# Gelu from PSUM, clip within the fp16 split, maxima by scans: the feed-forward of a conv/attention hybrid on one core

## The reference

```python
def _quantize_activations_groupwise(x):          # NUM_GROUPS = 5, EPS = 1e-5, QB = 128
    n = x.shape[0]
    gs = n // NUM_GROUPS
    xq = jnp.zeros_like(x)
    for g in range(NUM_GROUPS):
        ag = x[g * gs:(g + 1) * gs]
        gamma = jnp.max(jnp.abs(ag))
        xq = xq.at[g * gs:(g + 1) * gs].set(jnp.clip(ag * QB / (gamma + EPS), -QB + EPS, QB - EPS))
    return xq

def _bitlinear(x, W, b):
    Wb = _binarize_weights_groupwise(W)
    y = jnp.einsum('btc,oc->bto', x, Wb) + b
    return _quantize_activations_groupwise(y)

h = _bitlinear(x, W1, b1)                        # 192 -> 768
h = jax.nn.gelu(h, approximate=False)
out = _bitlinear(h, W2, b2)                      # 768 -> 192
...
t = t + _L1_ffn_ref(_ln_t(t), ...)
```

## Time and profile before

| | |
|---|---|
| median of 3 runs | 5051.42 us (5050.09 to 5053.39) |
| span of the profiled execution, first to last instruction | 5053.9 us |
| busy, TensorE / VectorE / ScalarE / GpSimd | 4182.5 / 3623.6 / 2966.6 / 773.5 us |
| mean granted clock of TensorE | 0.940 |
| all DMA queues | 161.72 MB, about 14% of 16 engines' span |

### The profile page before, as it was taken

The page is one execution under the profiler, slowest core; times in us unless marked ns, Lnnn a source line. Parts: engine busy times, 40 slices in busy tenths (PEclk is TensorE's granted clock), DMA queues, the critical chain, the costliest instruction groups (busy, mean ns, idle before and its releaser), DMA issues.

```text
span 5053.9 us, 119820 instructions
## 1 busy us (share of the span) xinstructions
PE 4182.5 (83%) x38848; PEld 3015.4 (60%) x38848; DVE 3623.6 (72%) x8151; ACT 2966.6 (59%) x6655; POOL 773.5 (15%) x671
## 2 busy tenths in 40 slices
PE   4989887879889876989897779889876988897777
PEld 2666664556666545666664556666545666664555
DVE  3767678767777786777778667677775777678666
ACT  1555556846555575555566746555575555566745
POOL 0000002600000143000002600000153000002600
PEclk8999998989999998999998989999998999998989
DMA  2111111011121101111111011211101111111011
GB/s 64 33 33 33 34 38 26 0 45 33 38 53 33 33 0 38 33 33 39 33 33 26 0 45 38 46 40 33 33 0 38 33 33 39 33 33 26 0 38 39
DMA packets 46393, 161.72 MB, mean 32 GB/s; under 512 B 10098, under 2 KB 10612, under 8 KB 45684
## 3 DMA queue, kind: packets, MB, share of 16 engines
q1 hardware_dynamic: 45812, 154.38, 13.0%
HBM read 28.52 MB, written 25.17 MB: 11 GB/s over the span
## 4 chain that ended last, share of the span: by engine, by line
issue 78%; POOL 13%; PE 5%; DVE 2%; POOLq 1%; ACT 0%; DMA 0%; SPq 0%; DVEq 0%; ACTq 0%
POOL work L483 7%; POOL hi_z L453 1%; POOL hi_z L472 1%; POOL rstd L448 1%; POOL rstd L468 1%; PE S L662 1%; POOL NK L443 1%; PE OUT L649 1%; PE PT L734 1%; PE PT L630 1%; DVE nmax L1082 0%; PE S L670 0%; DVE work L339 0%; DMA B<-in_b 0%; PE S L616 0%
## 5 line engine op out<-in xcount | busy, mean ns | idle before, releaser
L841 ACT ACTIVATE work<-S,nmax 128x128 f32<-128x128 f32 (+7 forms) x1536 | 1138.8, 742 | 1119.0 <-DVE nmax L1082 1112.1
L1082 DVE TENSOR_REDUCE nmax<-S 128x1 f32<-128x128 f32 (+7 forms) x1536 | 1155.4, 753 | 620.3 <-PE S L618 574.5
L630 PE MATMUL PT<-ident,work 128*128 128x128 f32 x6912 | 1089.2, 282 | 270.5 <-DVE work L339 246.9
L630 PEld LDWEIGHTS PT<-ident,work 128*128 128x128 f32 x6912 | 752.4, 142 | 493.6 <-DVE work L339 291.5
L339 DVE COPY work<-PT 128x512 f32<-128x512 f32 (+3 forms) x1536 | 893.1, 581 | 25.1 <-PE PT L630 19.4
L662 PE MATMUL S<-odd,W1b 128*128 (+1 forms) x2160 | 526.9, 400 | 71.4 <-DVE work L1155 64.1
L483 POOL TENSOR_TENSOR work<-work 128x512 f16<-128x512 f32 x360 | 414.0, 1158 | 148.4 <-ACT work L887 120.1
L662 PEld LDWEIGHTS S<-odd,W1b 128*128 128x128 f16 x2160 | 214.1, 102 | 354.4 <-DVE work L1155 94.8
L616 PE MATMUL S<-KS,QS 128*128 128x512 f16 (+3 forms) x1152 | 335.9, 347 | 103.5 <-issue 60.9
L443 POOL TENSOR_TENSOR NK<-NK,halfneg 96x4 f32<-96x4 f32 x32 | 32.5, 1016 | 2200.7 <-DVE NK L1007 2200.7
L845 ACT ACTIVATE work<-PT 128x512 f32<-128x512 f32 (+3 forms) x768 | 330.3, 430 | 57.1 <-PE PT L630 57.1
(11 more groups left out here) (189 smaller groups left out, 6718.5 us busy)
## 6 DMA issues: line engine op xcount, KB each, us to landing
X<-in_x SPq DMA_DIRECT2D x32, 768.0 KB, 5.3
odd<-hi_z SPq DMA_DIRECT2D x128, 192.0 KB, 4.1
odd<-odd SPq DMA_DIRECT2D x128, 192.0 KB, 4.2
out_y<-work SPq DMA_DIRECT2D x64, 384.0 KB, 3.1
QS<-hi_z SPq DMA_DIRECT2D x64, 192.0 KB, 3.5
QS<-odd SPq DMA_DIRECT2D x64, 192.0 KB, 4.0
KS<-hi_z SPq DMA_DIRECT2D x64, 192.0 KB, 4.6
KS<-odd SPq DMA_DIRECT2D x64, 192.0 KB, 4.5
```

The source lines that it names most:

```text
L630: last = tr(bank[:, P * (j - c0):P * (j - c0) + P], PS[m % 2][:, m // 2 % 2, P * j:P * j + P], ident[:, :])
L841: A(PS[n % 2][:, n // 2 % 2, 0:w], S[:, n % 2, 0:w], ACT.Exp, bias=nmax[:, n:n + 1], accum_out=rowsum[:, n:n + 1]).then_inc(exp_made, 1)
L1082: v.tensor_reduce(nmax[:, n:n + 1], S[:, n % 2, 0:P * (qtile(n) + 1)], AX.X, ALU.max, negate=True).then_inc(max_made, 1)
```

## The change

It touches the three passes in one edit.

- Pass 1: TensorE writes two 512-wide tiles of one `m` into one 1024-wide half of `S`, ScalarE takes the absolute value of 1024 at once into six slots of `JUNK`, and VectorE runs three scans an image (`tensor_tensor_scan` with maximum and maximum over two slots of `JUNK`) that carry one running maximum, whose last element is `run1`. The statistics of the next image stand ahead of the wait for the transposes, and all maxima stand behind the rounding.
- Pass 2: ScalarE applies Gelu straight from PSUM. VectorE then takes the minimum with 127.99999 twice over a pair of tiles, once into the fp16 tensor `HS` and once in place in `H`; a clip after Gelu gives the same values, as Gelu leaves values near 128 as they are and turns those near -128 into 0. GpSimd subtracts a pair of tiles at a time. The maxima of `Y2` go to a table, reduced once for the group.
- Pass 3: `OT` and `OS` get four slots, and the loops run over pairs of images.

```diff
-        JUNK = work[:, 0:512 * JR].rearrange("p (a b) -> p a b", a=JR)
-        OS = work[0:CH, 0:2048].rearrange("p (h c n) -> p h c n", h=2, c=2)
-        OT = work[:, 2048:2048 + 2 * 4 * C].rearrange("p (h n) -> p h n", h=2)
+        JUNK = work[:, 0:NTOK * MH].rearrange("p (a b) -> p a b", a=MH)
+        RUNMAX = work[:, NTOK * MH:NTOK * MH + NTOK]
+        run1 = work[:, NTOK * MH + NTOK - 1:NTOK * MH + NTOK]
+        OS = work[0:CH, 0:4096].rearrange("p (s c n) -> p s c n", s=4, c=2)
+        OT = work[:, 4096:4096 + 4 * 4 * C].rearrange("p (s n) -> p s n", s=4)
...
@@ gpsimd @@
-                    for i in range(2 * MH):
-                        pool.wait_ge(hhi_made, ab * 12 + (i + 1))
-                        hs = HS[:, i // MH, :, i % MH, :]
-                        pool.tensor_tensor(hs[:, 1, :], H[:, i % MH, :], hs[:, 0, :], ALU.subtract).then_inc(hlo_made, 1)
+                    for i in range(MH):
+                        hf, ms = i // 3, slice(2 * (i % 3), 2 * (i % 3) + 2)
+                        pool.wait_ge(hhi_made, ab * 12 + (2 * i + 2))
+                        pool.tensor_tensor(HS[:, hf, 1, ms, :], H[:, ms, :], HS[:, hf, 0, ms, :],
+                                           ALU.subtract).then_inc(hlo_made, 1)
...
@@ tensor @@
                 def y1(b, ab):
-                    for i in range(12):
-                        if i % 6 == 0:
-                            pe.wait_ge(z2t_made, ab * 4 + (2 + 2 * (i // 6)))
-                        if i >= 4:
-                            pe.wait_ge(abs_made, ab * 12 + (i - 3))
-                        ffn1(Z2[:, b, i // 6], Y[i % 4], i).then_inc(y1_full, 1)
+                    for m in range(MH):
+                        if m == 0:
+                            pe.wait_ge(z2t_made, ab * 4 + 4)
+                            alone(pe)
+                        pe.wait_ge(abs_made, ab * MH + (m + 1))
+                        for hf in range(2):
+                            last = ffn1(Z2[:, b, hf], S[:, m % 2, 512 * hf:512 * hf + 512], m)
+                        last.then_inc(y1_full, 1)
...
-                        if clips is not None or m >= 4:
-                            pe.wait_ge(clip_made, (ab * 12 if clips is None else clips) + (m - 3))
-                        ffn1(Z2[:, b, hf], Y[(MH * hf + m) % 4], m).then_inc(y_full, 1)
+                        i = MH * hf + m
+                        pe.wait_ge(gelu_made, ab * 12 + (i + 1))
+                        ffn1(Z2[:, b, hf], Y[i % 4], m).then_inc(y_full, 1)
...
@@ scalar @@
-                        A(JUNK[:, i % JR, :], Y[i % 4], ACT.Abs, bias=B1[:, i % 6:i % 6 + 1]).then_inc(abs_made, 1)
+                        A(JUNK[:, m, :], S[:, m % 2, :], ACT.Abs, bias=B1[:, m:m + 1]).then_inc(abs_made, 1)
...
-                        act.wait_ge(clip_made, ab * 12 + (i + 1))
-                        h = H[:, i % MH, :]
-                        A(h, h, ACT.Gelu, bias=rb1[:, i % 6:i % 6 + 1], scale=r1).then_inc(gelu_made, 1)
-                        if i:
-                            split_h(ab, i - 1)
-                    split_h(ab, 2 * MH - 1)
+                        act.wait_ge(y_full, ab * 12 + (i + 1))
+                        if i % 2 == 0:
+
+                            act.wait_ge(hlo_made, ab * MH + (i // 2 + 1))
+                        A(H[:, i % MH, :], Y[i % 4], ACT.Gelu, bias=rb1[:, i % MH:i % MH + 1],
+                          scale=r1).then_inc(gelu_made, 1)
...
@@ vector @@
-                def max_y1(ab, first, last):
-                    for i in range(first, last):
-                        dve.wait_ge(abs_made, ab * 12 + (i + 1))
-                        v.tensor_reduce(gm[:, i:i + 1], JUNK[:, i % JR, :], AX.X, ALU.max).then_inc(max1_step, 1)
...
+                def max_y1(ab, j):
+                    dve.wait_ge(abs_made, ab * MH + (2 * j + 4))
+                    alone(dve)
+                    dve.wait_ge(max1_step, ab * 3 + g + (j + 3))
+                    v.tensor_tensor_scan(RUNMAX, JUNK[:, 2 * j, :], JUNK[:, 2 * j + 1, :], run1, ALU.max,
+                                         ALU.max).then_inc(max1_step, 1)
...
+                    norm2(b1, ab1, "stats", range(TT))
                     dve.wait_ge(z2t_full, ab * 4 + 4)
                     alone(dve)
-                    norm2(b1, ab1, "stats", range(TT))
-                    max_y1(ab, 0, 4)
                     norm2(b1, ab1, "norm", range(TT))
                     norm2(b1, ab1, "round", halves[0])
                     norm2(b1, ab1, "round", halves[1])
-                    max_y1(ab, 4, 12)
-                max_y1(g * GS + (GS - 1), 0, 12)
+                    for j in range(3):
+                        max_y1(ab, j)
+                for j in range(3):
+                    max_y1(g * GS + (GS - 1), j)
...
-                        v.tensor_scalar(H[:, m, :], Y[i % 4], clip_hi[:, m:m + 1], clip_lo[:, m:m + 1],
-                                        ALU.min, ALU.max).then_inc(clip_made, 1)
+                def split_h(ab, hf):
+                    for p in range(3):
+                        ms = slice(2 * p, 2 * p + 2)
+                        dve.wait_ge(gelu_made, ab * 12 + (MH * hf + 2 * p + 6))
+                        if p == 0:
+                            alone(dve)
+
+                            dve.wait_ge(y2_full, ab * 4 + (2 * hf + 2))
+                        v.tensor_scalar(HS[:, hf, 0, ms, :], H[:, ms, :], QB - Q_EPS, None,
+                                        ALU.min).then_inc(hhi_made, 1)
+                        v.tensor_scalar(H[:, ms, :], H[:, ms, :], QB - Q_EPS, None, ALU.min).then_inc(hhi_made, 1)
...
-                with dve.Fori(0, GS) as b:
-                    ab = dve.snap(g * GS + b)
-                    for hf in range(2):
...
+                with dve.Fori(0, GS // 2) as b2:
+                    for u in range(2):
+                        b = dve.snap(b2 * 2 + u)
+                        ab = dve.snap(g * GS + b)
+                        for hf in range(2):
+
+                            dve.wait_ge(ot_full, ab * 2 + (hf + 1))
+                            v.tensor_scalar(OT[:, 2 * u + hf, :], Y2[:, b, hf, :], c2, c2n, ALU.min,
+                                            ALU.max).then_inc(o_step, 1)
```

More of the change, by code:

```diff
@@ L295, in hybrid_kernel @@
         os_made = sem("os_made")
-        stored = [sem(f"stored{i}") for i in range(2)]
+        stored = [sem(f"stored{i}") for i in range(4)]
         passed = sem("passed")
@@ L375, in front, with store @@
                                          srcs[part][32 * r:32 * r + 32, :, :]).then_inc(stacked[grp], 16)
-            def store(b, hf, n):
+            def store(b, s, n):
+                hf = s % 2
                 sp.wait_ge(os_made, n)
                 sp.dma_start(out[b].rearrange("(c p) n -> p c n", p=CH)[:, :, 512 * hf:512 * hf + 512],
-                             OS[:, hf, :, :]).then_inc(stored[hf], 16)
-            for hf in range(2):
-                sp.sem_inc(stored[hf], 16)
+                             OS[:, s, :, :]).then_inc(stored[s], 16)
+            for s in range(4):
+                sp.sem_inc(stored[s], 16)
             load_x(0)
@@ L391, in group_tail @@
             def group_tail(g):
-                with sp.Fori(0, GS) as b:
-                    for hf in range(2):
-                        store(g * GS + b, hf, g * (2 * GS) + b * 2 + (hf + 3))
+                with sp.Fori(0, GS // 2) as b2:
+                    for s in range(4):
+                        store(g * GS + b2 * 2 + s // 2, s, g * (2 * GS) + b2 * 4 + (s + 3))
             groups(sp, pair_body, group_tail)
             front(LAST, 1, False)
-            for u in range(2):
-                for hf in range(2):
-                    store(2 * LAST + u, hf, 4 * LAST + 2 * u + hf + 3)
-            for hf in range(2):
-                sp.wait_ge(stored[hf], 16 * (B + 1))
+            for s in range(4):
+                store(2 * LAST + s // 2, s, 4 * LAST + s + 3)
+            for s in range(4):
+                sp.wait_ge(stored[s], 16 * (B // 2 + 1))
         @block.gpsimd
@@ L596, in turn_z @@
                 return last
-            pe.sem_inc(ot_full, 2)
+            pe.sem_inc(ot_full, 4)
             pe.sem_inc(y2_full, 4)
@@ L1201, in group_tail @@
                 alone(dve)
[L1202 to L1211 removed]
+                with dve.Fori(0, GS // 2) as b2:
[6 more added lines that the diff above has]
+                                            ALU.max).then_inc(o_step, 1)
+                        for hf in range(2):
+                            dve.wait_ge(o_step, ab * 4 + (hf + 1))
+                            v.scalar_tensor_tensor(out=OT[:, 2 * u + hf, :], in0=OT[:, 2 * u + hf, :], scalar=r2,
+                                                   in1=T1H[:, b, hf, :], op0=ALU.mult, op1=ALU.add).then_inc(o_step, 1)
             groups(dve, pair_body, group_tail)
```

145 lines of the change are left out of this document (56 added, 89 removed).

## The result

The changed kernel takes 5145.14 us (median of 4 runs, 5141.42 to 5148.1), the kernel before in the same comparison 5052.41 us (4 runs, 5050.09 to 5057.66). The ratio is 1.0183, with a 95% interval of 1.0169 to 1.0198: 93 us slower. The forecast was 5170 us.

The account below looks back on a forecast made before the run. No engine is full in any feed-forward pass; a chain of engines sets each one's pace. Pass 1 +89, pass 2 +73, pass 3 -41 and end -2 give +119 us on 5051.4: 5170 us, range 5085 to 5225.

Parts of the forecast that it names:

- an uncovered power: Pass 1: with no maxima beside it, GpSimd's power is no longer hidden; statistics to normalisation takes 4.85 us.
- The scan's length and its exclusion: Pass 1: a scan takes 2.4 us and excludes GpSimd's subtraction, so VectorE stands still for 3.16 us an image.
- Rival A: Pass 1: the scan is fast, 1.3 us; round 15.3 us, 25 us instead of 89, time 5106; chance 0.11.
- the block: Pass 1: three scans with the time excluded by GpSimd's subtractions, 3 x 2.4 + 3.16 us a round.
- the head: Pass 1: from the start of the statistics to the end of the two casts, 8.10 us before the first scan.
- The total of pass 1: Pass 1 over all images: four full rounds at +4.4 plus 0.2, 17.8 us a group, +89 in five.
- Pass 2: VectorE's fast minima and GpSimd's subtractions run in turn, 3.3 us a pair; 20.6 us an image for 18.2; +73.
- rivals B: Pass 2: VectorE and GpSimd don't exclude each other, TensorE is the bound, 16.9 us an image; time 4995; chance 0.12.
- C: Passes 1 and 2: A and B both hold, the change at its best; pass 1 12.2 a round, time 4932; chance 0.05.
- D: Passes 1 and 2: worse turns, TensorE at lower clock, one us an image more in both; 5230; chance 0.11.
- Pass 3: Four output tiles let VectorE run two images ahead; 3.3 us an image for 5.2, 41 us less in five groups.
- The rest: At the program's end two waits for stores go, -2 us.

Follow-up runs that it names:

- The experiment with reductions: The changed kernel with six reductions of 128x1024 an image in place of the three scans, same order: 5097.2 us (1.0085 to the kernel before).
- the split on VectorE: The changed kernel with pass 2's minimum and difference in one VectorE operation and no GpSimd there: 4966.66 us (0.9834 to the kernel before).

## Why the prediction was right, and where it was not

The mechanisms that made the forecast were there: slow scans, an uncovered power, and VectorE's fast minima and GpSimd's subtractions in turn. How near the number came is in part luck, since in passes 1 and 2 rounds forecast too long stood against ends forecast too short.

**The scan's length and its exclusion: right.** I took 2.4 us for a scan; it is 2.35. I let it exclude GpSimd's subtraction and charged 3.16 us an image; it is 9.52 from the first scan to the next statistics, less 3 x 2.35, so 2.5. The experiment with reductions shows that it is exclusion. The subtraction doesn't come between two scans as a whole each time: it takes 5.37 us for two, of which 3.16 would be its own. Rival A (1.3 us) is out. The Trainium skill, "DVE: opcode table, instruction layouts, handler registers and perf-mode slots", section 6, has the built-in scan at half throughput; by it I had an estimate of 2.3 us, and the trace agrees with 2.35.

**The round of pass 1: 17.50 for 18.5 us.** Beside the block, the head is 7.99 (844.28 to 852.27) for my 8.10. Against 14.05 the round grows by 3.45: the uncovered power brings +2.1 (4.73 us from statistics to normalisation, where it was 5.11 with 2.46 of maxima in it), the block +2.5, and three scans in place of twelve reductions with their joins -1.1.

**The total of pass 1 came out right by luck: its errors cancel.** Predicted 17.8 us a group, measured 17.6 on average of the five. I let four rounds repeat in full at +4.4, less 0.5 for the first. Measured from rounding to rounding, only three repeat, at +3.45 each, which makes 10.4. The first two together cost +0.7, since the second image's statistics no longer wait for TensorE. The end was under-sized: I said +0.7 for the last image, but in the first group it is 28.1 us from the start of its rounding to the all-reduce (886.33 to 914.43), and before it was 21.9 (876.73 to 898.67): +6.2, and +6.6 on average. Of the 6.2, its matmuls start 3.5 later after the rounding: 2.0 because the scans hold up its second subtraction too, 1.5 because all four copies are awaited. The 36 matmuls then take 0.8 longer (granted clock 0.84 for 0.90), and from their end to the all-reduce, with an absolute value and a scan of 1024, it is 1.9 more. The step that failed is the one that took the last image's end from the kernel before. A small slip beside it: I let an image's matmuls end before its scans begin, but they end 0.6 us after (870.37 and 869.77); no scan waits for them in the repeating rounds.

**Pass 2: exclusion right, its pattern half right.** I forecast 3.3 us for a pair in turn, it is 3.14, and rivals B (16.9 a round) and C are out. So is D: TensorE's clock does fall, as D said (the last 48 matmuls take 6.70 us, with a granted clock of 0.50, 1.2 GHz, in the first 4.3 of them), but the rounds are shorter than forecast, not longer. The turns are not the ones I drew. I had both minima and then the subtraction in a row, and a first minimum stretched to 2 us; in the trace the first one of the next pair mostly slips in ahead of GpSimd, and it is the second that waits (2.61 for 0.68). In the first group's pass 2 that is so for 24 of 36 second minima, and for 5 of 36 first ones, of 1.90 and 2.70 us. Of the 1.3 us of VectorE that I counted in a pair 0.63 are on the path, and GpSimd's 2.12 are stretched by 0.39. The average of five rounds is 19.9 us (929.74 to 1029.27) for 18.1, so +8.8 where I had +12. The end was again too small: +2.6 predicted, +4.3 measured (3.1 for the last half, 1.2 for matmuls at a lower clock), and the head +1.3 for 0. That makes 14.4 us in this group, and 13.1 on average, for my 14.6: here too a round too long and ends too short nearly cancel.

The Trainium skill, "SBUF — State Buffer", section "Who interferes with whom", has the rule by which VectorE at a fast two-port pace, or with two inputs from SBUF, and GpSimd block each other for a whole instruction. The traces agree: L1143 (2.61 us for 0.68) and the scans (3.69 for 2.35) are stretched, or stretch GpSimd's subtractions; the reductions (six in 6.85 us), and the minima with one operand in PSUM and no fast pace (1.21 to 1.23), are not. By the same section issue order decides who is blocked, and the trace agrees: 0.16 us of lead give L1141 the turn at 980.27.

**Pass 3: too careful.** I took 3.3 us an image from TensorE's clock in that stage (0.66). With four tiles TensorE waits 1.03 us for 1.89 between two images, its clock is 0.83 on average, 16 transposes take 2.00 us, and VectorE's 3.04 us is the bound. That gives -47.8 instead of -41, well inside my bounds of -18 and -54.

**The rest: -15.8 for -2.** This term, which I had set at two waits, holds 14 of the 29 us by which the sum is too high. Four stretches of attention between the feed-forward parts are 9.4 us shorter, though nothing was changed there. Some 6 of that are a matter of the profiled execution of before: from the second all-reduce to the next pass 1 it has 717.5, 719.5, 717.7 and 723.0 us, the kernel with pass 2 alone changed has 717.8 each time. In the changed kernel it is 706 to 708, some 0.7 a group more than pass 3 itself gains. The last pair and the end give 5.9. Why attention behind a shorter pass 3 gains this I haven't tested; it stays open.

**A cost that both kernels have and I had not read.** The wait of the all-reduces stood in the trace of before as idle time put down to "issue", and I took it as fixed. It doesn't touch the difference between the two kernels, but it accounts for 28 (5 x 5.7) of the 98 us by which the expectation for the split on VectorE missed.

## What to carry to other kernels

Before work is moved to a fast VectorE form or to an operation with two SBUF inputs, look at what GpSimd does at that moment: here the two then ran in turn, and a slower form with an operand in PSUM, or VectorE alone, can be faster (17.5 and 16.2 us for 20.1 here). When operations are merged, check what the old ones were hiding: one reduction of 1.22 us in the right place was worth some 30 us, a part of it through TensorE's clock. And read "issue" ahead of an all-reduce on GpSimd: where subtractions stood before it, an early call that nobody awaits, in time in which GpSimd is idle, took some 5.6 us off the path each time.

## What the hardware showed that I had not expected

- GpSimd took 5.64 us from a subtraction's end to the start of an all-reduce whose input had long been there, but started 0.2 us after VectorE's result when the last thing it ran was an all-reduce. The Trainium skill, "GPSIMD Engine Reference", section 2.1 "Instruction dispatch", has about 6 us (5.95 measured) for the first call to a freshly loaded routine, with no instruction in the profile for it. The trace agrees in size, though no run here shows that it is such a loading; that the price comes back after every stretch of subtractions, ten times in this kernel, and that it can be paid early is what these runs add.
- An instruction that is held up shows as a longer instruction and not as idle time: the groups of the changed kernel have L1143 at a mean of 1970 ns and no idle time ahead of it, and VectorE "busy" 120.0 of 139.8 us in pass 2, though the same minima take 0.68 us alone.

```profile
L1143 DVE TENSOR_SCALAR work<-work 128x1024 f32<-128x1024 f32 x180 | 354.6, 1970 | 0.0
```
